# Edge loop of a graph network: features of two tiles per weight load, and what moves with it

## The reference, cut to what matters

```python
def _mlp(x, W0, b0, W1, b1, g, b):
    h = jax.nn.silu(x @ W0 + b0)
    return _ln(h @ W1 + b1, g, b)
e = _mlp(mesh2grid_efeat, emb_W0, emb_b0, emb_W1, emb_b1, emb_g, emb_b)     # 4 attributes per edge
e_in = jnp.concatenate([e, mesh_nfeat[src], grid_nfeat[dst]], axis=-1)
e_new = _mlp(e_in, edge_W0, edge_b0, edge_W1, edge_b1, edge_g, edge_beta) + e
agg = jax.ops.segment_sum(e_new, dst, num_segments=grid_nfeat.shape[0])
```

## Time and profile before

| | |
|---|---|
| median of 3 runs | 2457.78 us (2457.52 to 2460.72) |
| profiled execution, its own time | 2459.82 us |
| its span, first to last instruction | 2458.1 us |
| busy: PE, DVE, ACT, GpSimd | 2267.3, 1410.5, 1180.5, 1100.8 us |
| counting stage | 304 to 427 us |
| edge loop | 793 to about 2333 us |

### The profile page before, as it was taken

One profiled execution on the slowest core, in us unless ns is written; L12 is line 12 of the kernel. 1 busy time (PEld: TensorE's weight loads), 2 busy tenths in 40 slices (PEclk: granted clock), 3 DMA queues, 4 the chain that ended last, 5 costly groups with the idle time before them and its releaser, 6 DMA issues. The chain is left out here.

```text
span 2458.1 us, 44265 instructions
## 1 busy us (share of the span) xinstructions
PE 2267.3 (92%) x13412; PEld 1922.2 (78%) x13413; DVE 1410.5 (57%) x3090; ACT 1180.5 (48%) x2123; POOL 1100.8 (45%) x1665
## 2 busy tenths in 40 slices
PE   2988488999986899999999999999999999999897
PEld 1436388777764788888888888888888888888776
DVE  7012288534462566666666666666666666666566
ACT  0121111324311666666666666666666666666421
POOL 4777600000001455555555555555555555555323
PEclk9999799999998899999999999999999999999899
DMA  6223100001123433333233333233333333323121
GB/s 191 78 54 79 19 0 1 34 5 35 35 89 115 133 61 60 63 64 60 60 60 60 64 61 63 60 60 60 63 60 61 62 60 61 63 60 65 24 91 43
DMA packets 76277, 149.67 MB, mean 61 GB/s; under 512 B 14689, under 2 KB 15789, under 8 KB 76219
## 3 DMA queue, kind: packets, MB, share of 16 engines
q0 software_dynamic: 44864, 93.18, 19.8%
q1 hardware_dynamic: 31243, 55.63, 6.8%
q10 hardware_dynamic: 112, 0.11, 0.0%
HBM read 129.12 MB, written 19.46 MB: 60 GB/s over the span
## 5 line engine op out<-in xcount | busy, mean ns | idle before, releaser
L1277 DVE CUSTOM_DVE_ANT_0 c_var_bank<-c_var_bank,c_p,k_floor 128x512 f32<-128x512 f32 x176 | 133.5, 758 | 369.4 <-PE c_var_bank L1434 369.4
L1168 POOL DMA_INDIRECT c_from_src<-s_dst_table,c_at_nodes x176 | 283.8, 1613 | 31.9 <-issue 31.9
L1488 PE MATMUL c_edge_bank<-c_m_hi,c_pt_hi 128*128 128x512 f32 x704 | 291.7, 414 | 0.0
L1489 PE MATMUL c_edge_bank<-c_m_lo,c_pt_hi 128*128 128x512 f32 x704 | 276.8, 393 | 0.0
L1490 PE MATMUL c_edge_bank<-c_m_hi,c_pt_lo 128*128 128x512 f32 x704 | 275.2, 391 | 0.0
L1162 POOL DMA_INDIRECT c_from_src<-s_mesh_table,c_at_nodes x176 | 206.3, 1172 | 152.1 <-POOL c_at_nodes L1158 142.8
L1174 POOL TENSOR_TENSOR c_dev<-c_var,k_half 128x1 f32<-128x1 f32 x176 | 97.8, 556 | 383.9 <-DVE c_var L1264 383.9
L318 POOL DMA_INDIRECT s_records<-a_stage_rec,a_stage_row x170 | 207.3, 1219 | 56.8 <-issue 48.8
L1383 ACT ACTIVATE c_h<-c_from_src 128x512 f32<-128x512 f32 x176 | 111.2, 632 | 249.0 <-DVE c_from_src L1296 249.0
L1432 PE MATMUL c_var_bank<-c_m_hi,c_pt_hi 128*128 128x384 f32 x704 | 226.6, 322 | 4.5 <-ACT c_var_bank L1357 4.5
L1432 PE MATMUL c_var_bank<-c_m_hi,c_ht_hi 128*128 128x384 f32 x704 | 226.8, 322 | 0.0
(11 more groups left out here) (313 smaller groups left out, 6023.0 us busy)
## 6 DMA issues: line engine op xcount, KB each, us to landing
k_w<-in_L_gnn_Ws_self_dram SPq DMA_DIRECT2D x3, 1024.0 KB, 10.1
k_w<-in_L_gnn_Ws_neigh_dram SPq DMA_DIRECT2D x3, 1024.0 KB, 12.8
c_from_src<-s_mesh_table,c_at_nodes POOLq DMA_INDIRECT x176, 3.5
c_from_src<-s_dst_table,c_at_nodes POOLq DMA_INDIRECT x176, 4.7
s_records<-a_stage_rec,a_stage_row POOLq DMA_INDIRECT x170, 2.6
a_mesh<-in_L_gnn_mesh_nfeat_dram SPq DMA_DIRECT2D x10, 250.0 KB
k_h<-in_x_dram SPq DMA_DIRECT2D x1, 2500.0 KB
s_mesh_table<-a_mesh_out SPq DMA_DIRECT2D x10, 250.0 KB
```

The source lines that it names most:

```text
L1168: pool.indirect_dma_start(from_src[u][:], None, scratch["dst_table"], bass.IndirectOffsetOnAxis(ap=at_nodes[u][:, 1:2], axis=0), compute_o ...
L1277: dve.tensor_tensor_reduce(var1_bank[:], var1_bank[:], p[u % 2][:], 1.0 / D, k["floor"][:, 0:1], ALU.mult, ALU.add, var[u][:, 0:1]).then_i ...
L1488: pe.matmul(edge_bank[:], left[0], m_hi[1][:, c, :], start=False, stop=False, skip_group_check=True)
L1489: pe.matmul(edge_bank[:], left[0], m_lo[1][:, c, :], start=False, stop=False, skip_group_check=True)
```

## The change

Features of a pair of tiles (2m, 2m+1) are made at once, in the odd step before the pair, with 256 columns per weight load, into two banks: the first two chunks in one, the others in the second. There is one `w0` now, with the 14 rows at all four positions, and instead the attributes are spread out, each tile in its own 128 columns and 32 rows, the rest zero, by four ACT copies. ACT makes the Silus of the front bank and of the first tile's half of the back bank in the odd step; the second tile's half (`hidden_rest`) is left for the next, even step. The bank that this needs is that of the small sums, which go, tile by tile, into eight columns of the turn bank and are added up by DVE in SBUF (`add_r`). ACT's and DVE's orders change, and the counting stage gets one gate per bank. The diff, cut:

```diff
@@ open_gates @@
-            engine.wait_ge(copied_out, engine.value_load(k["tile_bucket1"][0:1, ds(2 * i + u, 1)], min_val=1, max_val=NB))
-            engine.sem_inc(gate[u], 1)
+            bucket1 = engine.value_load(k["tile_bucket1"][0:1, ds(2 * i + u, 1)], min_val=1, max_val=NB)
+            for b in range(3):
+                engine.wait_ge(copied_out[b], bucket1)
+                engine.sem_inc(gate[b][u], 1)
...
@@ phase_a, scalar @@
             for b in range(3):
                 lo, hi = b * 512, min((b + 1) * 512, NB * P)
-                act.activation(k["adj"][:, c, lo:hi], bank[b][:, 0:hi - lo], ACT.Copy)
-            act.activation(k["degree"][:, c:c + 1], bank[3][:, 0:1], ACT.Copy).then_inc(copied_out, 1)
+                act.wait_ge(count_mm[b], done)
+                last = act.activation(k["adj"][:, c, lo:hi], bank[b][:, 0:hi - lo], ACT.Copy)
+                if b == 2:
+                    last = act.activation(k["degree"][:, c:c + 1], bank[3][:, 0:1], ACT.Copy)
+                last.then_inc(copied_out[b], 1)
...
@@ phase_a, tensor, count @@
+            for b, blocks in enumerate((range(4), range(4, 8), range(8, NB))):
+                pe.wait_ge(gate[b][u % 2], n // 2 + 1 if fixed else (n - u % 2 + 2) // 2)
+                for s in blocks:
+                    last = pe.matmul(bank[b][:, (s % 4) * P:(s % 4 + 1) * P], hot_src[u][:, s * P:(s + 1) * P], hot_dst[u][:],
+                                     start=False, stop=False, skip_group_check=True)
...
+                last.then_inc(count_mm[b], 1)
...
@@ phase_c @@
-    sum_p_bank, sum_h_bank, sum_r_bank = psum("sum_p_bank"), psum("sum_h_bank"), psum("sum_r_bank")
+    feat_bank = [psum(f"feat_bank{i}") for i in range(2)]
...
+    tile_r = turn_bank[:, P:P + 8]
...
-    w0 = [sb(f"w0_{u}", [P, D], F32R) for u in range(GROUP)]
+    w0 = sb("w0", [P, D], F32R)
...
-    attr_t = [sb(f"attr_t{i}", [P, P], F32R) for i in range(2)]
+    attr_t = [sb(f"attr_t{i}", [P, GROUP * P], F32R) for i in range(2)]
+    fresh, sum_now = sb("fresh", [P, TILES]), sb("sum_now", [P, 8])
...
@@ vector @@
+        def add_r(n):
+
+            dve.wait_ge(sums_mm, n + 1)
+            need(dve, sum_now_ok, n)
+            dve.scalar_tensor_tensor(out=sum_now[:], in0=sum_now[:], scalar=at(fresh, n), in1=tile_r,
+                                     op0=ALU.mult, op1=ALU.add).then_inc(sum_now_ok, 1)
...
@@ leave @@
-                dve.wait_ge(sums_mm, n + 1)
+                dve.wait_ge(sum_now_ok, n + 1)
                 dve.sem_inc(tick, 1)
+                dve.tensor_copy(tile_of(k["sum_r"], b), sum_now[:])
                 dve.tensor_copy(tile_of(k["sum_p"], b), sum_p_bank[:])
...
-                dve.memset(sum_h_bank[:], 0.0)
-                dve.memset(sum_r_bank[:, 0:8], 0.0).then_inc(sums_left, 1)
+                dve.memset(sum_h_bank[:], 0.0).then_inc(sums_left, 1)
...
@@ vector, step @@
             n = GROUP * i + u
+            if exists(n - 3):
+                add_r(n - 3)
...
-            if exists(n - 2):
-                low_rh(n - 2, (u - 2) % 4)
             if exists(n + 1):
                 low_p(n + 1, (u + 1) % 4)
             if exists(n - 1):
                 low_ht(n - 1, (u - 1) % 4)
             if exists(n - 3):
                 leave(n - 3)
+            if exists(n - 2):
+                low_rh(n - 2, (u - 2) % 4)
...
@@ scalar @@
         def turn_out(g, v):
             act.wait_ge(stack_turned, g + 1)
-            act.activation(attr_t[v][:], turn_bank[:, 0:P], ACT.Copy).then_inc(attr_t_ok, 1)
+            for u in range(GROUP):
+                part = slice(STK * u, STK * (u + 1))
+                last = act.activation(attr_t[v][part, u * P:(u + 1) * P], turn_bank[part, 0:P], ACT.Copy)
+            last.then_inc(attr_t_ok, 1)
...
+            need(act, pt_lo_ok, n)
+            need(act, edge_mm, n - 2)
+            front, back = (b[:].rearrange("p (k n) -> p k n", k=2) for b in feat_bank)
             act.wait_ge(pt_mm, n + 1)
...
+            act.activation(pt_hi[u // 2][:, 0:2, :], front, ACT.Silu)
+            act.activation(pt_f[:, 0:2, :], front, ACT.Silu).then_inc(front_ok, 2)
+            act.wait_ge(pt_mm, n + 2)
+            act.activation(pt_hi[u // 2][:, 2:4, 0:P], back[:, :, 0:P], ACT.Silu)
+            act.activation(pt_f[:, 2:4, 0:P], back[:, :, 0:P], ACT.Silu).then_inc(first_ok, 2)
+
+        def hidden_rest(n, u):
+
+            back = feat_bank[1][:].rearrange("p (k n) -> p k n", k=2)
+            act.activation(pt_hi[u // 2][:, 2:4, P:2 * P], back[:, :, P:2 * P], ACT.Silu)
+            act.activation(pt_f[:, 2:4, P:2 * P], back[:, :, P:2 * P], ACT.Silu).then_inc(second_ok, 2)
...
@@ scalar, step @@
+            if u == 2 and exists(n + 2):
+                need(act, sum_now_ok, n - 2)
+                turn_out(i + 1, 1 - v)
+            if u % 2 and exists(n + 1):
+                hidden(n + 1, (u + 1) % 4)
+            if u % 2 == 0:
+                hidden_rest(n + 1, u + 1)
             if exists(n + 1):
-                hidden(n + 1, (u + 1) % 4)
+                hidden_rows(n + 1, (u + 1) % 4)
             if exists(n - 1):
+                high_ht(n - 1, (u - 1) % 4)
                 need(act, var2_ok, n - 1)
                 bias_into(var2_bank, 2, var2_set)
             if exists(n - 2):
                 high_rh(n - 2, (u - 2) % 4)
...
@@ tensor @@
         def features(n, v, u):
+
             need(pe, p_ok, n)
+            need(pe, second_ok, n)
...
+                last = pe.matmul(feat_bank[c // 2][:, (c % 2) * 2 * P:(c % 2 + 1) * 2 * P], w0[:, c * P:(c + 1) * P],
+                                 attr_t[v][:, u * P:(u + 2) * P], start=True, stop=True, skip_group_check=True)
+                if c % 2:
+                    last.then_inc(pt_mm, 1)
...
@@ turn_h @@
+            need(pe, sum_now_ok, n - 1)
...
@@ sums @@
-            pe.matmul(sum_r_bank[:, 0:8], hot[u][:], dev_parts[u][:], start=False, stop=False,
-                      skip_group_check=True).then_inc(sums_mm, 1)
+            need(pe, sum_now_ok, n)
+            pe.matmul(tile_r, hot[u][:], dev_parts[u][:], start=True, stop=True, skip_group_check=True).then_inc(sums_mm, 1)
...
@@ tensor, step @@
-            if exists(n + 1):
+            if u % 2 and exists(n + 1):
                 features(n + 1, after, (u + 1) % 4)
```

More of the change, by code:

```diff
@@ L200, in phase_a @@
     mesh_turned, mesh_t_ok, mesh_mm, mesh_ok = (sem(n) for n in ("mesh_turned", "mesh_t_ok", "mesh_mm", "mesh_ok"))
-    hot_ok, count_mm, counts_out = sem("hot_ok"), sem("count_mm"), sem("counts_out")
-    copied_out = sem("copied_out")
-    gate = [sem(f"gate{i}") for i in range(2)]
+    hot_ok = sem("hot_ok")
+    count_mm = [sem(f"count_mm{b}") for b in range(3)]
+    copied_out = [sem(f"copied_out{b}") for b in range(3)]
+    gate = [[sem(f"gate{b}_{i}") for i in range(2)] for b in range(3)]
     bias_in, w_hi_ok, w_lo_ok, hc_ok, hc_turned, ht_hi_ok, ht_lo_ok = (
@@ L669, in count @@
             pe.wait_ge(hot_ok, n + 1)
[L671 to L678, removed]
+            for b, blocks in enumerate((range(4), range(4, 8), range(8, NB))):
[3 more added lines that the diff above has]
+                                     start=False, stop=False, skip_group_check=True)
+                if b == 2:
+                    last = pe.matmul(bank[3][:, 0:2], hot_dst[u][:], ones16[:], start=False, stop=False,
+                                     skip_group_check=True)
+                last.then_inc(count_mm[b], 1)
+        for b in range(3):
+            pe.sem_inc(copied_out[b], 1)
         for u in range(GROUP):
@@ L1217, in _ @@
         dve.memset(zeros16[:], 0.0)
-        for u in range(GROUP):
-            dve.memset(w0[u][:].bitcast(F32), 0.0).then_inc(w0_zero, 1)
-        dve.wait_ge(w0_zero, GROUP)
+        dve.memset(w0[:].bitcast(F32), 0.0).then_inc(w0_zero, 1)
+        for v in range(2):
+            dve.memset(attr_t[v][:].bitcast(F32), 0.0)
+        dve.memset(sum_now[:], 0.0)
+        dve.memset(fresh[:, 0:1], 1.0)
+        dve.tensor_scalar(fresh[:, 1:], k["tile_last"][:, 0:TILES - 1], 0.0, None, ALU.is_equal).then_inc(w0_zero, 1)
+        dve.wait_ge(w0_zero, 2)
         dve.memset(stack[:, :, A4:A4 + 1], 1.0)
@@ L1306, in _ @@
         last = TILES - 1
+        add_r(last - 2)
         low_ht(last, 3)
@@ L1310, in _ @@
         variance2(last, 3)
+        add_r(last - 1)
         leave(last - 1)
         low_rh(last, 3)
+        add_r(last)
         leave(last)
@@ L1342, in hidden_rows @@
             need(act, rp_lo_ok, n - 1)
-            act.activation(p[u % 2][:], feat_bank[:], ACT.Silu).then_inc(p_ok, 1)
+            act.activation(p[u % 2][:], feat_bank[0][:], ACT.Silu).then_inc(p_ok, 1)
         def high_rh(n, u):
@@ L1377, in step @@
             act.activation(rp_hi[u][:], p[u % 2][:], ACT.Copy, scale=dev[u][:, 0:1]).then_inc(rp_hi_ok, 1)
-            if u == 1 and exists(n + GROUP):
-                turn_out(i + 1, 1 - v)
             act.wait_ge(z_ok, n + 1)
@@ L1501, in _ @@
```

(2 more changed lines are left out.)

63 lines of the change are left out of this document (30 added, 33 removed).

## The result

The changed kernel takes 2435.35 us (median of 4 runs, 2429.51 to 2436.19), the kernel before 2459.25 beside it (4 runs). The ratio is 0.9897, 95% interval 0.9879 to 0.9916: faster by 24 us, where 50 were predicted. The direction was right; the time lies 0.35 us outside the range, and half of the gain is missing.

The account below looks back on a forecast made before the run. PE's work was taken to bound the edge loop, DVE and bucket hand-overs the counting. 40 + 4.4 + 6.6 less 1 gave 50 us off 2459.82, 2409.8, said as 2408 for the median; 8-in-10 range 2397 to 2435.

Parts of the forecast that it names:

- What bounds the kernel: Edge loop: PE's own work is the time, so a removed matmul is worth its full pitch; counting: DVE and bucket hand-overs.
- Part 1: Edge loop, features of two tiles per weight load: 0.45 us saved per pair, 88 pairs, 40 us; bounds 32 and 47.
- Part 2: Edge loop, low_rh behind low_ht so low_ht comes earlier: 0.1 us in one step of four, 4.4 us, bounds 0 and 5.
- Part 3: Edge loop, PE's added semaphore waits: taken as hidden, cost 0, bounds 0 and 22 us.
- Part 4: Edge loop, ACT's additional Silu and turn_out instructions: fit in margins of about 0.3 us, cost 0, upper bound 44 us.
- Part 5: Sums in SBUF and nine inner bucket ends: no difference in PE's wait, bounds -3 and +4 us in all.
- Part 6: Counting stage, a gate per count bank: 0.7 us at each of 9 bucket changes plus 0.3, 6.6 us; bounds 0 and 8.5.
- a late engine takes back half: Rival, edge loop: ACT margins missed by 0.25 us each odd step, or PE's new waits show, 22 us: 2430; chance 0.15.
- the gate loops: Rival, counting stage: SP's and POOL's three register waits each repeat a 1.0 us round, 153 us more: 2568; chance 0.05.
- 2420 for cheaper matmuls: Rival, edge loop: removed feature matmuls save only 0.32 us per pair, 38 us in all; chance 0.05.
- 2419 for gates and reorder doing nothing: Case where count gates and DVE's reordering gain nothing, 2408 + 11; counted within the forecast's own range, no separate chance.

Follow-up runs that it names:

- low_rh late: The kernel before with only DVE's low_rh (which makes c_hot) moved from the front of its step to behind the leave: 2468.68 against 2457.07, ratio 1.0047.
- the control: The changed kernel unaltered, run again as the measure for follow-up kernels: 2431.20, ratio to the kernel before 0.9892.
- low_rh in front: The changed kernel with DVE's low_rh put back ahead of low_p, low_ht and the leave, everything else of the change kept: 2681.52, ratio to the kernel before 1.0910.
- the load hoisted: The changed kernel with PE's load of the bucket number issued ahead of the three waits of the sums: 2418.11, ratio to the kernel before 0.9835.

## Why the prediction was half right

1. **What bounds the kernel**: right. PE sets the edge loop, and its removed time came off one for one within the buckets.
2. **Part 1, features**: right. From the kernel before with low_rh late to the change, four steps go from 33.95 to 33.07, 0.44 per pair against my 0.45: 39 us of 40. No run has the pairing alone, so this difference also holds ACT's new order, add_r and the new waits, whose own worth in a step was taken as 0; the gates by themselves leave the steps as they were (34.10). The 0.32 that I had put beside it, after the Trainium skill (TensorE: Matmul & The Clock Gate, section "Back-to-back issue gap"), would have been 28; the trace decides for the pitch of 0.11 to 0.12.
3. **Part 2, the stall of ht_lo**: right in kind, 6.2 us instead of 4.4, a little beyond my bound of 5. It needs ACT's new order as well once the features are paired, which I didn't say.
4. **Part 3, PE's new waits**: right, 0. The even steps are 0.45 to 0.56 shorter with the waits in them.
5. **Part 4, ACT**: right within what it claimed. PE waits for attr_t 0.4 us once in some of the traces, and for c_pt_f once late in the loop, 0.8 at 2167. I did miss that high_rh moved, and with it that DVE's order was tied to it.
6. **Part 5, bucket ends: the step that failed.** "I take no difference, bounds -3 and +4 us in all", on the ground that hot comes after the leave "while the leave itself begins 0.8 earlier". It measured +21 (28.7 against 8.1), or +16 in the control. I had balanced the leave against itself and left out who is last then. The leave did begin earlier, but by 0.44 and not 0.8: 2.52 us after PE's turn of h (966.63, 964.11) against 2.96. c_hot had been made before the leave and was no part of the wait; now it is ready 0.77 behind the leave's last memset (970.03, 969.26). And the bucket number's load, hidden before because the sequencer ran ahead, is bare once the semaphore in front of it is late: the first sum follows its releaser by 1.19 now (971.22, 970.03) and followed it by 0.05 (977.02; the small memset of 976.90 lasts 0.07). 0.77 + 1.14 - 0.44 = 1.47, and the gap went from 0.46 to 1.96, 1.50 more; most of the 0.03 left is the leave, 0.05 longer. A gap of 2 us can then have a second price, the clock. The nine gaps are 13 us longer in sum (16.9 against 4.0) and six falls at 1.55 are 9; that is 22, of which some 2 come off again in the steps at and behind the ends, for 21. The rows for this were there: c_hot's place in DVE's order, and the order of waits and load in the source.
7. **Part 6, gates**: 4.8 us off the stage and 2.9 (0.5 to 5.4) off the kernel instead of 6.6. At the change of bucket, PE goes on at 329.29 where it was 330.44, and DVE still idles:

```profile
329.29 1.11 PE L676 MATMUL a_bank<-a_hot_dst,a_hot_src 128*128 128x128 bf16 x10 [0.39 <-SPq L221]
```

```profile
330.59 0.55 DVE L484 TENSOR_SCALAR a_hot_src<-a_src_grid,k_recs 128x1280 bf16<-128x1280 int16 x1 [0.25 <-PE a_bank L679]
```

0.91 became 0.25, so 0.66 of the 0.7 that I took at this change; the nine together gave 4.8 / 9 = 0.53. The mechanism stands, the size was some 2 us too large. How much of it survives until the edge loop isn't settled: the loop's first 8-column sum matmul stands at 832.54 before, at 828.95 in the trace with low_rh late, which has no gates, at 829.71 with the gates alone, and at 829.25 and 826.85 in two executions of the changed kernel.

**The sum as it came out**, in the profiled execution: 39 + 6 (within buckets) + 5 (gates, in their stage) - 21 (ends) = 29; the profiled times differ by 23.6. The traces show where the other 5 went, if not why. Between the counting stage and the loop's first sum it is 1.4 (the stage gained 4.7, the first sum stands 3.3 earlier), less than two executions of one kernel differ by there. In the loop, away from the bucket ends, it is some 2: one step's wait for c_pt_f (0.8 on its row) and the loop's last three steps, 1.2 slower against their medians than before. Behind the last sums it is 1.3.

The rivals: "a late engine takes back half" had the right size and sign and the wrong place (each odd step instead of nine ends); the gate loops did not slow; 2420 for cheaper matmuls and 2419 for gates and reorder doing nothing were not what happened.

## What to carry to other kernels

When a producer is moved behind a rare block of work, look at that rare step by itself: who was last there, who is last now, and what stands in the queue of the engine behind its wait, loads of a register above all; load a register that doesn't depend on a wait ahead of it. A gap of about 2 us on TensorE can cost another 1.5 in clock, as it did in half of the cases here. Where an order is changed on one engine, read the same items' order on the engine that feeds it before calling it separate.

## What the runs showed of the hardware that I had not expected

- **Gap and clock.** From 930 to 2200 us of twelve traces, none of the 76 gaps of PE between 0.25 and 1.4 us was followed by a fall of the clock, and none of 137 more in the kernel with low_rh in front, where most are 1.25 to 1.35. Of ten from 1.5 to 1.7, two were, and of 30 from 1.87 to 2.21, fifteen. A fall takes 1.71 us of clock each time, and made a bucket's end 1.50 to 1.57 us longer. Why one of two equal gaps is followed by it, the traces don't show.
- **A register load on PE's queue** took 296 to 324 ns where the sequencer ran ahead (before, and with the load hoisted). Bare behind the wait for c_hot it took 607 to 875 ns at six of the change's nine ends and 303 to 306 at three. In both kernels the register operation after it (0.15) began 0.06 after its end. Why the load is longer at some bare places isn't settled; no register load of another engine overlapped it in the traces.
- **A second register load in DVE's step** cost 6.2 us over 176 steps (2417.03 - 2410.81; 7.9 by the ratios to the kernel before, 0.9838 and 0.9806), on an engine that is busy 61% of the time in the changed kernel. It shows as about one step in eight being 0.2 longer and the third of four 8.68 instead of 8.63. What in the load does it, no run shows.
